# The shared expert's first chunk of 512 tokens moves from inside the second attention to behind it

## The reference, cut to what matters

```python
def _clamped_swiglu(x, wg, wu, wd):
    g = jnp.clip(x @ wg.T, -ALPHA, ALPHA)
    u = jnp.clip(x @ wu.T, -ALPHA, ALPHA)
    return jax.nn.silu(g) * u @ wd.T
...
logits = flat @ router_w.T
scores = jnp.sqrt(jax.nn.softplus(logits))
_, idx = jax.lax.top_k(scores + expert_bias, K)
...
out, _ = jax.lax.scan(body, jnp.zeros_like(flat), (gate_w, up_w, down_w, probs.T))
out = out + _clamped_swiglu(flat, shared_gate_w, shared_up_w, shared_down_w)
```

## Time and profile before

| | us |
|---|---|
| runs | 646.13, 653.28, 654.76 (median 653.28) |
| profiled execution, its own time | 649.37 |
| its span | 647.6 |
| second attention, first score of sequence 4 to the last division | 336 to 428 |
| behind it, up to the first block of the expert loop | 428 to 471 |

### The profile page before, as it was taken

How to read it: one execution, slowest core, us unless ns; L and a number is a source line. 1 busy time by engine, 2 the same in 40 slices (tenths; PEclk the granted TensorE clock), 3 DMA queues, 4 the chain that set the end, 5 groups by cost and what they waited for, 6 DMA issues and landing times.

```text
span 647.6 us, 14149 instructions
## 1 busy us (share of the span) xinstructions
PE 557.5 (86%) x4202; PEld 397.7 (61%) x4203; DVE 431.6 (67%) x1296; ACT 352.7 (54%) x902; POOL 243.1 (38%) x341
## 2 busy tenths in 40 slices
PE   4999898799879789898988987884689999889986
PEld 2565465466458764576756755552567787777864
DVE  4558787688236886676787773452757777767855
ACT  2452476577736578356665546442146665556662
POOL 2353010000603213275545534476525555445530
PEclk9999699899999889999999987798789999989999
DMA  7499879400000006777214151163335454434499
GB/s 249 162 302 284 232 197 271 128 4 2 3 1 1 2 0 179 226 208 229 117 63 171 69 212 68 57 222 148 115 108 149 147 151 144 143 118 147 147 362 343
DMA packets 49536, 95.21 MB, mean 147 GB/s; under 512 B 8580, under 2 KB 40524, under 8 KB 46924
## 3 DMA queue, kind: packets, MB, share of 16 engines
q1 hardware_dynamic: 41804, 75.34, 37.7%
q0 software_dynamic: 7680, 19.21, 7.9%
HBM read 58.54 MB, written 35.59 MB: 145 GB/s over the span
## 4 chain that ended last, share of the span: by engine, by line
PE 45%; DVE 20%; issue 11%; POOL 8%; DMA 7%; ACT 6%; another core or an unknown queue 1%; DVEq 0%; ACTq 0%; POOLq 0%; SPq 0%
PE banks L1423 6%; PE banks L1379 5%; PE banks L1240 4%; POOL rows_by_expert L890 4%; PE banks L1444 4%; DVE mx L1943 3%; PE banks L1315 3%; PE banks L1624 3%; DVE mx L1940 3%; POOL results_by_rank L926 3%; DMA arena<-negT 3%; DVE attn_w L2137 2%; PE banks L1246 2%; DMA arena<-results_by_rank 2%; PE banks L1635 2%
## 5 line engine op out<-in xcount | busy, mean ns | idle before, releaser
L1095 ACT ACTIVATE arena<-banks 128x512 f32<-128x512 f32 (+1 forms) x256 | 130.1, 549 | 88.7 <-PE banks L1423 50.4
L926 POOL DMA_INDIRECT results_by_rank<-attn_w,goes x80 | 78.1, 976 | 82.8 <-issue 49.7
L1423 PE MATMUL banks<-arena 98*128 98x256 bf16 (+1 forms) x512 | 90.5, 271 | 18.1 <-DMA arena<-negT 5.5
L1940 DVE TENSOR_REDUCE mx<-banks 128x4 f32<-128x1024 f32 x64 | 76.1, 1221 | 21.7 <-PE banks L1379 21.6
L1379 PE MATMUL banks<-arena 96*128 96x256 bf16 (+1 forms) x512 | 83.0, 267 | 5.4 <-DVE mx L1940 2.5
L890 POOL DMA_INDIRECT rows_by_expert<-arena,bpb x64 | 63.5, 992 | 59.1 <-ACT arena L1095 26.4
L1624 PE MATMUL banks<-arena,attn_w 128*128 x320 | 84.7, 388 | 0.3 <-issue 0.3
L1423 PEld LDWEIGHTS banks<-arena 98*128 98x128 bf16 x512 | 44.4, 102 | 52.0 <-ACT arena L1095 16.7
L1943 DVE TENSOR_REDUCE mx<-banks 128x4 f32<-128x1024 f32 (+1 forms) x48 | 57.5, 1221 | 20.3 <-PE banks L1383 19.4
L1379 PEld LDWEIGHTS banks<-arena 96*128 96x128 bf16 x512 | 50.6, 100 | 21.6 <-issue 5.6
L1624 PEld LDWEIGHTS banks<-arena,attn_w 128*128 128x128 f32 x320 | 55.9, 195 | 5.3 <-issue 0.9
(11 more groups left out here) (246 smaller groups left out, 1107.8 us busy)
## 6 DMA issues: line engine op xcount, KB each, us to landing
arena<-parts_dram SPq DMA_DIRECT2D x72, 256.0 KB, 4.0
pvs<-rows_by_expert SPq DMA_DIRECT2D x80, 130.0 KB
parts_dram<-arena SPq DMA_DIRECT2D x24, 384.0 KB, 3.0
arena<-results_by_rank SPq DMA_DIRECT2D x6, 1024.0 KB, 10.4
arena<-in SPq DMA_DIRECT2D x2, 2304.0 KB
rows_by_expert<-zero SPq DMA_DIRECT2D x1, 4160.0 KB, 23.4
arena<-in SPq DMA_DIRECT2D x2, 1920.0 KB
arena<-in SPq DMA_DIRECT2D x3, 768.0 KB
```

What stands on the lines that cost most here:

```text
L926: pool.indirect_dma_start(ys, bass.IndirectOffsetOnAxis(ap=goes[:, j:j + 1], axis=0), yb[j], None).then_inc(y_stored[j], 16)
L1095: act.activation(p_ring[n][:, i % P_RING, :], st_bank[RING_AT[n]["s", b, s] % 3][:, 0:P_WIDTH[n]], ACT.Exp, scale=HD ** -0.5).then_inc(exp ...
L1423: ins = pe.matmul(dst[:, at:at + SEQ - q0], keys, q_rows(n, slice(0, ROWS), s, b, q0, SEQ - q0), start=True, stop=(n == 0 or b < POOL_MASKS))
L1940: ins = dve.tensor_reduce(out, src.rearrange("p (q h k) -> p q h k", q=QT, k=nk), AX.X, ALU.max)
```

## The change

`shared_up(0)` to the addition of chunk 0 are taken out of the steps of the attention. Behind it, all four chunks follow with the same code: chunk 0 takes the places of chunk 1, chunk 1 those of chunk 2 and so on, and one more round stands at the end. `shared_add` is gone: chunk 0 gets the four products with the identity and `copy_added(0)`. Two loads of ScalarE's function table in the attention (the one at L1054 and the one at L1111) are gone with it.

```diff
-UP_AT, CLIP_AT, TANH_AT, HIDDEN_AT, DOWN_AT, ADD_AT = ((6, 7), (6, 9)), (6, 10), (7, 1), (7, 7), ((7, 9), (7, 11)), (7, 12)
...
@@ scalar, attention @@
-                        if n and (b, s) == TANH_AT:
-                            shared_tanh(0)
-                            act.preload_act_table_set(EXP_AND_LN)
@@ scalar, behind it @@
-            shared_tanh(1)
+            shared_tanh(0)
             copy_rows(SEQS - 1)
             soften(len(BATCHES) - 1)
             root_of_soft(len(BATCHES) - 1)
+            copy_added(0)
+            act.preload_act_table_set("exp_and_others")
+            shared_tanh(1)
             copy_added(1)
-            act.preload_act_table_set("exp_and_others")
             shared_tanh(2)
             shared_tanh(3)
             copy_added(2)
@@ tensor, shared_down @@
-                        ins = pe.matmul(dst, sh[:, at0:at0 + P], wsh[:, 2 * KD * INNER:EW], start=True, stop=(c == 0))
-                        if c:
-                            ins = pe.matmul(dst, ident[:, :], x[:, c * CT + 2 * j + t, :], start=False, stop=True)
+                        pe.matmul(dst, sh[:, at0:at0 + P], wsh[:, 2 * KD * INNER:EW], start=True, stop=False)
+                        ins = pe.matmul(dst, ident[:, :], x[:, c * CT + 2 * j + t, :], start=False, stop=True)
@@ tensor, attention @@
-                        if n and (b, s) in UP_AT:
-                            pe.wait_ge(shared_loaded, 16)
-                            shared_up(0, (UP_AT.index((b, s)),))
-                        if n and (b, s) in DOWN_AT:
-                            shared_down(0, (DOWN_AT.index((b, s)),))
                 values(n, SEQS * ROUNDS - 1)
                 turn_back(n, SEQS - 1)
                 if n:
+                    pe.wait_ge(shared_loaded, 16)
+                    shared_up(0)
                     shared_up(1)
-                    shared_up(2)
                     turn_rows(SEQS - 1)
                     logits(len(BATCHES) - 1)
                     ranks(len(BATCHES) - 2)
+                    shared_down(0)
+                    shared_up(2)
+                    ranks(len(BATCHES) - 1)
+                    count()
                     shared_down(1)
                     shared_up(3)
-                    ranks(len(BATCHES) - 1)
-                    count()
+                    spread()
                     shared_down(2)
-                    spread()
                     shared_down(3)
@@ vector, attention @@
-                        if n and (b, s) == CLIP_AT:
-                            shared_clip(0)
-                        if n and (b, s) == HIDDEN_AT:
-                            shared_hidden(0)
...
-                        if n and (b, s) == ADD_AT:
-                            shared_add(0)
@@ vector, behind it @@
                 divide(n, SEQS - 1)
                 if n:
-                    shared_clip(1)
+                    shared_clip(0)
                     top_four(len(BATCHES) - 2)
                     pick_four(len(BATCHES) - 2)
-                    shared_hidden(1)
+                    shared_hidden(0)
                     read_logits(len(BATCHES) - 1)
                     find_slots(len(BATCHES) - 2)
+                    shared_clip(1)
                     add_soft(len(BATCHES) - 1)
                     top_four(len(BATCHES) - 1)
                     pick_four(len(BATCHES) - 1)
+                    find_slots(len(BATCHES) - 1)
+                    shared_hidden(1)
                     shared_clip(2)
-                    find_slots(len(BATCHES) - 1)
-                    shared_hidden(2)
...
+            count_blocks()
+            shared_hidden(2)
             shared_clip(3)
-            count_blocks()
+            place_blocks()
             shared_hidden(3)
-            place_blocks()
```

More of the change, by code:

```diff
@@ L333, in two_block_kernel @@
         slots_e = cut(arena, SMALL + 3 * most, most, tile_expert, t=most // EXPERTS)
-        grow = cut(arena, SMALL + 4 * most, most, tile_expert, t=most // EXPERTS)
         part = cut(arena, SMALL + 4 * most, most * TOPK, "p (t k e) -> p t k e", t=most // EXPERTS, k=TOPK)
@@ L1519, in spread, with shared_up @@
                 ins.then_inc(spread_ready, 1)
-            def shared_up(c, parts=(0, 1)):
+            def shared_up(c):
                 if c >= 2:
@@ L1525, in shared_up @@
                     pe.wait_ge(unit_done[1], SEQS * len(PAIRS[1]))
-                for j in parts:
+                for j in range(2):
                     for k in range(KD):
@@ L1530, in shared_up, with shared_down @@
                                         xnT4[:, k, c * CHUNK:(c + 1) * CHUNK], start=(k == 0), stop=(k == KD - 1))
-                if j == 1:
-                    ins.then_inc(sgu_ready, 1)
-            def shared_down(c, parts=(0, 1)):
+                ins.then_inc(sgu_ready, 1)
+            def shared_down(c):
                 pe.wait_ge(shid_ready, c + 1)
-                for j in parts:
+                for j in range(2):
                     for t in range(2):
@@ L1869, in shared_hidden @@
                                          ).then_inc(shid_ready, 1)
-            def shared_add(c):
-                for j in range(2):
-                    dve.wait_ge(sdown_ready, 2 * c + j + 1)
-                    xt = x[:, c * CT + 2 * j:c * CT + 2 * j + 2, :]
-                    dve.tensor_tensor(xt, xt, bank[2 * (c % 2) + j][:, :].rearrange("p (t d) -> p t d", t=2), ALU.add
-                                      ).then_inc(sdown_added, 1)
             rows, upto, over, these = (cnt[i] for i in range(4))
```

## The result

| | before | after |
|---|---|---|
| median, 20 runs each | 650.31 us | 655.24 us |
| lowest, highest | 645.59, 656.82 | 648.79, 662.68 |
| ratio after to before, 95% interval | | 1.0076 (1.005 to 1.0101) |
| span of the profiled execution | 647.6 | 652.0 |
| sequence 6 | 24.2 | 24.1 |

A sequence is counted from the exponential of step 15 of the sequence before it to its own step 15, in all runs alike: 373.8 and 398.0 in the earlier trace rows are such times, and the first exponentials of sequences 6 and 7 themselves stand at 374.4 and 399.2.

A forecast was written before the change was run, and what follows sets the result against it. The prediction took sequences 6 and 7 of the attention, with chunk 0 in their chains, and the 43.6 us behind as what changes. It summed -9.7 + 1.7 = -8.0 us from 650.9 to 643 us, range 638 to 648.

The forecast's parts named there:

- items 2 to 4: Attention: removing chunk 0's tanh frees 2.6 us, its down product's first half 3.6, the second half 1.1.
- remote: Behind the attention: the trace's word for what held find_slots(4) idle 10.53 us after ranks(4); its return was the largest unknown.
- the rival that the attention doesn't shorten: Attention: division, normalising and router beside chunk 0 are the true chain; no own chance, included in the low end.
- Item 1: Attention, sequence 6: removing the up product's two halves, 3.86 us of TensorE, gives back 2.4 us.
- item 2: Attention: removing chunk 0's tanh and its two table loads gives back 2.6 us, bounds 1.3 and 3.3.
- The row without a drain: Attention: trace shows a 1.28 us table load without the skill page's 1.38 us drain, which would add up to 2.7.
- the 2.7 us for the lower clock: Behind the attention: added for TensorE products at 1.2 GHz after idling, moving the first block's start to 473.0.
- The first rival: Behind the attention: the stall at ranks(4) comes again at full length, +8 against -9.7, 649 us; chance 25%.
- The second rival: Chain behind the attention grows 10 to 13 us at 1.2 GHz, attention gives 6 to 9: 655 us; chance 12%.
- the third rival: Behind the attention: GpSimd stays last link, tail shrinks 3.6 us, attention gives 12.9: 634.5 us; chance 18%.

The follow-up runs named there:

- the kernel with two memsets: Changed kernel with two small GpSimd memsets, each waited for, behind every scatter, so scatters start 1.53 us apart: ratio to before 1.0013.
- 60 scatters in a row: Changed kernel with the 40 scatters of batches 0 to 2 moved behind the attention: 706.3 us, ratio 1.0835.
- one memset: Changed kernel with one small GpSimd memset behind scatters, which start 1.36 us apart: 658.9 us, ratio 1.0155.
- the order mended: Changed kernel with two memsets behind every scatter and scale_rows at step 5 instead of 8 in GpSimd's list: 642.5 us, ratio 1.0145.
- the kernels with gaps: Changed kernel and kernel before, two memsets behind every scatter: 1.0013 and 1.0023; with scale_rows earlier too, 1.0145 and 1.014.

## Why the prediction was wrong

**The attention, -9.7 forecast, -0.8 measured.** Each term was read as idle time that would go, and the rows of its stage were read rightly: with no scatter in the attention, sequence 7 loses 8.4 us where items 2 to 4 gave 7.3 (bounds 4.5 to 9.0). The step that failed is the one ahead of them, that sequence 7 waits in chains of which chunk 0 is the longest. Taking out its parts one by one gave back 0.7 us at most (31.1 and 29.1 us against 29.8), and taking it out wholly 2.4 (27.4). What stood in its place depends on GpSimd's scatters, as the 8.4 us without them show. In the profiles it is first the chain over late completions, which lay hidden under chunk 0's own waits. But with that lateness gone and the scatters still there the two kernels differ there by 0.3 and 0.2 us, so lateness alone is not the whole of it: the waits for GpSimd's `shift` and the lower clock are seen beside it, and how the loss is shared out is open. I took "remote" for one stall at `ranks(4)`, and wrote that the other `ranks` show nothing of the kind; the completions of values and scores near 385 and 402 were 2.4 and 2.0 us late in the kernel before, and were not looked for. I also set ScalarE's 3.89 us of idle time at the down product against 0.3 between plain steps, and so put aside the rival that the attention doesn't shorten. The same profile has 3.01 us in sequence 6, where TensorE has the router's products ahead of the scores and nothing of chunk 0:

```profile
395.37 0.49 ACT L1095 ACTIVATE arena<-banks 128x384 f32<-128x384 f32 x1 [3.01 <-PE banks L1426]
```

That rival had no chance of its own ("included in the low end"), and in its outcome it is what happened.

**Item 1, 2.4 us, has the wrong sign.** It priced the products by their records and by ScalarE's steps. What they cost is less than what their absence costs: sequence 6 takes 24.1 at a mean clock of 0.71 without them and 21.1 at 1.00 with them. Even with the scatters gone their absence gives -0.5. I weighed the clock behind the attention and not inside it.

**The table load.** The row without a drain stood: the tanh starts 0.01 us behind the load. But without the two loads sequence 7 took 31.1 us against 29.8, so the 2.6 us of item 2 weren't on the path.

**The stretch behind, +1.7 forecast, +5.8 measured.** The chain is the one written down, link by link: `copy_added(0)`, up(2), `ranks(4)`, hidden, down(1), up(3), spread, two downs, last copy, first block. Its first link was to be done 14.1 us behind the last division and was done 21.8 us behind it, since the message of down(0) was 7.9 us late; in the kernel with two memsets, without the lateness, it was done 14.9 us behind. Of the 7.7 us 4.1 were left at the end, as up(2) to up(3) ran tighter than forecast and the 2.7 us for the lower clock weren't needed (1.00 from 452 on). `find_slots(4)` and the first scatter of batch 4 waited in the changed kernel as in the earlier trace rows, but behind the late copy and up(2), for a `ranks(4)` that was itself on time:

```profile
454.76 0.22 DVE L2006 SCALAR_TENSOR_TENSOR arena<-iota,banks 128x64 f32<-128x64 f32 x1 [11.06 <-PE banks L1498]
```

```profile
456.38 1.15 POOL L888 DMA_INDIRECT rows_by_expert<-arena,bpb  x1 [6.09 <-DVE bpb L2014]
```

The first rival (the stall comes again, 25%) has the mechanism of this stretch, one link too late: it put the stall at `ranks(4)`, and it came at down(0). It gave +8 here and kept the attention's 9.7, hence 649 us. The second rival (12%) named 655 us, which is the time measured, and that is luck: it had the stretch grow by 10 to 13 us at 1.2 GHz throughout and the attention give 6 to 9, and the measured are 5.8, at 2.4 GHz from 452 on, and 0.8. One sum against the third rival doesn't come out: the chain is said to be 5 us longer than the scatters "even without a slow product"; from the prediction's own numbers it is 470.3 against 471.33 - 3.6 = 467.7, so 2.6, and 5.3 only with the slow products.

**What is open.** Profiles show the lateness directly; for unprofiled executions only the times speak. With 60 scatters in a row the changed kernel took 701.1 to 707.1 us without a profile and 708.0 with one. From the last scatter to the first block it was 7.0 us in the kernel before (464.31 to 471.33) and 27.4 here (502.70 to 530.13), so this wait at least must be in the unprofiled ones too. Which path TensorE's messages share with GpSimd's indirect DMAs no view shows. One hint: the program asks for 16 updates of a semaphore for each of its 64 scatters, 1024 in all, and the trace has records of 403 of them in the changed kernel, of 447 with one memset, 696 with two, 987 with the order mended, and 157 with 60 scatters in a row. Five profiles with (nearly) the kernel before's instructions behind the attention took 43.5 to 50.4 us there, so the 5.8 us between the two profiles are in part chance: the five with the changed one's (in one of them `spread` earlier) took 48.0 to 50.7, on average 2.7 more. And the kernels with gaps lose 1.4% on one chip and 0.2% on another, for which I have no profile of the kernel before.

## What to carry to other kernels

Before a stall is priced as idle time that goes, look in the chain of waits and in the completion times for a second stall under it, above all one that ends with another engine's work. Work taken away from TensorE in a stretch that it nearly fills can lower its clock and cost more than it took. Where GpSimd issues indirect DMAs back to back, look for late completions of TensorE. Other work between them ended the lateness here, but it made GpSimd's chain longer and no kernel faster (1.0013 to 1.0242 times the kernel before); what other engines wait for belongs in front of them.

## What the hardware showed

- Behind three or more indirect DMAs of GpSimd in a row, 1.27 us apart, TensorE's completions reach the other engines late: 160 of 197 by over 0.3 us, up to 5.2 us in the attention, 13.5 us behind it and 67.7 us with a row of 60. Behind one or two it is 122 of 568, behind none 0 of 263. In the seven kernels with starts 1.5 us or more apart (but for batch 4 in two of them) none of some 820 was over 1 us late. Of some 2100 completions of VectorE and ScalarE in the ten profiles counted above none was over 0.1 us late. The Trainium skill (SBUF — State Buffer, Who interferes with whom) says of the ports of that memory that DMA never contends with a compute engine. Nothing here speaks against it: by their records and the clock the products themselves were made in time. What is late is the message, and for the engine that waits this is the same.
- 3.86 us of dense products more in sequence 6 went with a clock of 2.4 GHz over all of its 21.1 us; without them it took 24.1 us at a mean of 0.71 (on one chip 24.7 at 0.73).
